# Two-layer AdaLN/MoE block on one core: index loads, ring depth, token layout and the sharing of the head's work

## The reference

```python
x = x + L0_ffn(L0_cond(x, cond))
x = x + L1_ffn(L1_cond(x, cond))

# L0_cond: per sample, a gate picks 2 of 4 experts
gate_in = [mean over all tokens | over head and proprio | over wrist and proprio]
mod = silu(cond) @ time_w + time_b                  # scale, shift
scores = softmax((gate_in @ gate_w + gate_b) * (1 + scale) + shift)
w_be = the two largest scores of the sample, normed to sum 1
for e in range(4):
    y = gelu_tanh(x @ ew1[e] + eb1[e]) @ ew2[e] + eb2[e]     # 128 -> 512 -> 128
    out += w_be[:, e] * mask[e] * y                          # mask: which tokens
out += gelu_tanh(x @ sw1 + sb1) @ sw2 + sb2                  # shared expert

# L0_ffn: all 8 experts, 128 -> 512 -> 128, silu(x @ w_gate) * (x @ w_up) @ w_down,
#         weighted by softmax(router) * softmax(gating / 0.1), normed
# L1_cond: 2 shared experts, 8 routed ones (top 2 of a sigmoid), 128 -> 128 -> 128
# L1_ffn: low rank, gelu(x @ U1 @ V1 + b1) @ U2 @ V2 + b2
```

## Time and profile before

| what | us |
|---|---|
| median of three runs | 980.28 |
| lowest, highest | 978.11, 985.54 |
| the profiled execution, whole | 976.85 |
| its span, first to last instruction | 975.1 |
| PE busy | 906.2 |
| DVE, ACT, POOL busy | 711.7, 564.0, 385.8 |

### The profile page before, as it was taken

The page is one execution under the profiler, slowest core; times in us unless marked ns, Lnnn a source line. Parts: engine busy times, 40 slices in busy tenths (PEclk is TensorE's granted clock), DMA queues, the critical chain, the costliest instruction groups (busy, mean ns, idle before and its releaser), DMA issues.

```text
span 975.1 us, 13047 instructions
## 1 busy us (share of the span) xinstructions
PE 906.2 (93%) x3862; PEld 718.9 (74%) x3862; DVE 711.7 (73%) x1096; ACT 564.0 (58%) x972; POOL 385.8 (40%) x355
## 2 busy tenths in 40 slices
PE   6887777788999999999999999999999999999997
PEld 4665555566788888888888888888888778777884
DVE  6765565564778786866866867768666698898988
ACT  5554444454665554555555555555555658898896
POOL 3602343331134556423523534435222315773551
PEclk8899999996999999999999999999999999999999
DMA  7256676740211131110011011101100019283840
GB/s 272 109 157 184 203 229 203 201 143 1 79 46 76 44 123 54 44 76 11 34 76 44 1 76 43 66 11 44 44 18 26 1 27 174 66 159 57 173 98 33
DMA packets 47671, 85.94 MB, mean 88 GB/s; under 512 B 4208, under 2 KB 26608, under 8 KB 45680
## 3 DMA queue, kind: packets, MB, share of 16 engines
q1 hardware_dynamic: 47600, 85.10, 29.9%
HBM read 68.57 MB, written 6.55 MB: 77 GB/s over the span
## 4 chain that ended last, share of the span: by engine, by line
PE 72%; SPq 8%; DVE 5%; issue 5%; DMA 4%; ACT 4%; POOL 0%; POOLq 0%; DVEq 0%; ACTq 0%
PE ps L772 15%; PE ps L777 15%; PE ps L787 15%; PE ps L817 7%; PE ps L824 7%; PE ps L822 7%; SPq L638 3%; DMA GWU<-expert_weights 3%; SPq L633 2%; PE ps L804 2%; PE ps L802 2%; DVE HL L1304 1%; ACT HH L906 1%; SPq L630 1%; PE ps L698 1%
## 5 line engine op out<-in xcount | busy, mean ns | idle before, releaser
L900 ACT ACTIVATE Sg<-ps 128x512 f32<-128x512 f32 x288 | 172.3, 599 | 250.1 <-PE ps L787 248.8
L1285 DVE TENSOR_TENSOR Hf<-ps,Sg 128x512 f32<-128x512 f32 x288 | 198.0, 688 | 150.6 <-ACT Sg L900 96.6
L1383 POOL TENSOR_TENSOR HL<-Hf,HH 128x512 fp32r<-128x512 f32 x130 | 174.0, 1345 | 165.0 <-ACT HH L906 152.9
L906 ACT ACTIVATE HH<-Hf 128x512 fp32r<-128x512 f32 x346 | 215.9, 624 | 12.8 <-DVE Hf L1285 7.4
L1304 DVE TENSOR_TENSOR HL<-Hf,HH 128x512 fp32r<-128x512 f32 x242 | 217.1, 897 | 4.3 <-ACT HH L906 3.3
L772 PE MATMUL ps<-XHL,WBH 128*128 128x512 f32 x512 | 204.5, 399 | 1.7 <-DVE Hf L1285 1.7
L787 PE MATMUL ps<-XHL,WBH 128*128 128x512 f32 x512 | 202.5, 396 | 0.0
L777 PE MATMUL ps<-XHL,WBL 128*128 128x512 f32 x512 | 202.5, 395 | 0.0
L1402 POOL TENSOR_TENSOR XT<-XT,TMP 128x512 f32<-128x512 f32 x64 | 83.5, 1305 | 255.3 <-DVE TMP L1190 255.3
L1304 DVE TENSOR_TENSOR HL<-ps,HH 128x512 fp32r<-128x512 f32 x120 | 82.6, 691 | 83.5 <-ACT HH L906 80.9
L772 PEld LDWEIGHTS ps<-XHL,WBH 128*128 128x128 f32 x512 | 96.4, 188 | 25.5 <-DVE Hf L1285 3.0
(11 more groups left out here) (242 smaller groups left out, 1383.6 us busy)
## 6 DMA issues: line engine op xcount, KB each, us to landing
CWB<-scratch SPq DMA_DIRECT2D x68, 256.0 KB, 6.8
CWB<-scratch SPq DMA_DIRECT2D x15, 1024.0 KB, 4.6
GX<-XHL SPq DMA_DIRECT2D x76, 128.0 KB, 2.8
GWU<-expert_weights SPq DMA_DIRECT2D x19, 512.0 KB, 3.6
GWD<-expert_weights SPq DMA_DIRECT2D x19, 512.0 KB, 4.9
ST<-in_wb_dram SPq DMA_DIRECT2D x8, 768.0 KB, 6.4
XT<-in_x_dram SPq DMA_DIRECT2D x8, 256.0 KB, 6.2
expert_weights<-GWU SPq DMA_DIRECT2D x4, 512.0 KB, 2.6
```

The costliest lines, as they stand in the source:

```text
L900: e.activation(Sg[:, it.n % NG, :], zb[z % NZ][:, :], ACT.Silu).then_inc(s_act, 1)
L906: e.activation(HH[:, it.n % NH, 0:it.cols], hidden_place(it), ACT.Copy).then_inc(s_hi_act, 1)
L1285: e.tensor_tensor(Hf[:, it.n % NS, :], zb[z % NZ][:, :], Sg[:, it.n % NG, :], ALU.mult).then_inc(s_prod, 1)
L1383: e.tensor_tensor(HL[:, it.n % NH, :], Hf[:, it.n % NS, :], HH[:, it.n % NH, :].bitcast(F32), ALU.subtract).then_inc(s_lo_pool, 1)
```

## The change

- Token parts lie beside each other: `XHL` is [block, part, 512] in place of [part, block, 512], and while it holds x it is used as `XS`, [sample, part, 128], so that both parts of a sample are one run of 1,024 B. `GX` has the same form.
- `GX`, `GWU`, `GWD` become rings of three (`NR`); `GP` is gone: its biases and the mask stand behind the weights in DRAM rows (`wup_d` rows of 1028 numbers, `wdown_d` of 1153), put there by two DRAM-to-DRAM copies in the head.
- `index` is [group, 9]: four samples for the copies, the expert, and four places for the additions. Numbers are loaded four at a time, without a range check, one group ahead; unused places of a group add to spare columns of `AC` (`AC` has 36 samples' width in place of 32), and the waits between POOL's additions are gone.
- The head: Silu is computed with tanh; a small gelu at the very start loads the table of the head; POOL takes ACT's casts of the expert weights; ACT takes the end of A units 0 to 5 from DVE (line 1169 before) and casts the high part of three of four A and G items in place of one of two; the small inputs come in two transfers; the sums over x stand one in each of slots 4 to 9; the other steps of `gates` move to other slots; the loads may begin at slot 19.
- `route_a`: blocks 0 to 3 together at slot t_g + 3 (before: 0, 1 at t_g + 2, 2, 3 at t_g + 3), blocks 4, 5 at t_g + 7 (before t_g + 6).
- `Hf` and `Sg` change places in memory.

The diff, cut to its core:

```diff
-PK = 133
+UROW = 1024 + 4
+DROW = 1024 + 1 + P
+NR = 3
...
-        XHL = sb("XHL", [P, 2, NBLK, BLK], F32R)
-        XH, XL = XHL[:, 0, :, :], XHL[:, 1, :, :]
+        XHL = sb("XHL", [P, NBLK, 2, BLK], F32R)
+        XH, XL = XHL[:, :, 0, :], XHL[:, :, 1, :]
+        XS = XHL[:, :, :, :].rearrange("p b a (s t) -> p (b a s t)", t=P).rearrange("p (s a t) -> p s a t", a=2, t=P)
         sm = sb("sm", [P, SMALL])
...
-        index = sb("index", [P, NPAIR + NGRP], mybir.dt.int32)
+        index = sb("index", [P, NGRP, 9], mybir.dt.int32)
...
-        GX = sb("GX", [P, 2, 2, BLK], F32R, actx)
-        AC = sb("AC", [P, NBLK, BLK], F32, actx)
+        GX = sb("GX", [P, NR, 4, 2, P], F32R, actx)
+        AC = sb("AC", [P, NB + 4, P], F32, actx)
         WAS = sb("WAS", [P, 2, 2, 512], F32R, actx)
-        GWU = sb("GWU", [P, 2, 2, 512], F32R, actx)
-        GWD = sb("GWD", [P, 2, 2, 512], F32R, actx)
-        GP = sb("GP", [P, 3, PK], F32, actx)
+        GWU = sb("GWU", [P, NR, UROW], F32R, actx)
+        GWD = sb("GWD", [P, NR, DROW], F32R, actx)
...
-        route_a = {t_g + 2: (0, 1), t_g + 3: (2, 3), t_g + 6: (4, 5), t_a[6] + 5: (6,), t_a[7] + 3: (7,)}
+        route_a = {t_g + 3: (0, 1, 2, 3), t_g + 7: (4, 5), t_a[6] + 5: (6,), t_a[7] + 3: (7,)}
...
-        first_load = 20
+        first_load = 19
...
-            it.hi_act = it.kind in "BS" or (it.kind in "AGF" and it.k % 2 == 1) or (it.kind == "R" and it.ex % 4 != 3)
+            it.hi_act = it.kind in "BS" or (it.kind in "AG" and it.k % 4 != 0) or (
+                it.kind == "F" and it.k % 2 == 1) or (it.kind == "R" and it.ex % 4 != 3)
...
-        load_x = {pos["G", g - 2, 0, 3].k + 1: g for g in range(2, NGRP)}
-        load_d = {pos["G", g - 2, 0, 3].k + LAG + 1: g for g in range(2, NGRP)}
+        load_x = {pos["G", g - NR, 0, 3].k + 1: g for g in range(NR, NGRP)}
+        load_d = {pos["G", g - NR, 0, 3].k + LAG + 1: g for g in range(NR, NGRP)}
...
-            e.dma_start(sm[:, :], small_d).then_inc(f_sm, 16)
+            e.dma_start(sm[:, 0:SOON], small_d[:, 0:SOON]).then_inc(f_sm, 16)
...
+            e.dma_start(sm[:, SOON:SMALL], small_d[:, SOON:SMALL]).then_inc(f_sm2, 16)
+            e.dma_start(wup_d[:, :, 1024:UROW], pack_d[:, :, 0:4]).then_inc(f_pack, 16)
+            e.dma_start(wdown_d[:, :, 1024:DROW], pack_d[:, :, 4:133]).then_inc(f_pack, 16)
...
-                    w = GWD if h else GWU
+                    d = wdown_d if h else wup_d
+                    w = (GWD if h else GWU)[:, (i - 1) % NR, 0:1024]
                     e.wait_ge(s_wa_lo, 2 * i + h)
-                    e.dma_start(wex_d[i - 1, h], w[:, (i - 1) % 2, :, :].rearrange("p a n -> p (a n)").bitcast(
-                        F32)).then_inc(f_wex[(i - 1) % 2], 16)
+                    e.dma_start(d[i - 1, :, 0:1024], w.bitcast(F32)).then_inc(f_wex[(i - 1) // NR], 16)
                 if k == first_load:
-                    e.wait_ge(s_index, 1)
                     e.wait_ge(s_x_hi, NBLK)
                     e.wait_ge(s_x_lo, NBLK - 1)
-                    e.wait_ge(f_wex[0], 64)
-                    e.wait_ge(f_wex[1], 64)
-                    for g in range(2):
-                        load_tokens(e, g)
-                        load_up(e, g)
-                        load_down(e, g)
+                    e.wait_ge(f_wex[0], 96)
+                    e.wait_ge(f_wex[1], 32)
+                    e.wait_ge(f_pack, 32)
+                    e.wait_ge(s_index, 1)
+                    found = [sources(g) for g in range(NR)]
+                    for g in range(NR):
+                        load_tokens(e, g, found[g])
+                        load_up(e, g, found[g])
+                        load_down(e, g, found[g])
+                    found.append(sources(NR))
                 if k in load_x:
                     g = load_x[k]
-                    e.wait_ge(s_z, pos["G", g - 2, 0, 3].z[0] + 1)
-                    load_tokens(e, g)
-                    load_up(e, g)
+                    e.wait_ge(s_act, pos["G", g - NR, 0, 3].n + 1)
+                    load_tokens(e, g, found[g])
+                    load_up(e, g, found[g])
+                    if g + 1 < NGRP:
+                        found.append(sources(g + 1))
                 if k in load_d:
                     g = load_d[k]
...
+        def indices(engine, g, a, b, most):
+
+            _, v = nc.values_load_multi_w_load_instructions(
+                index[0:1, g, a:b], engines=(engine,), min_val=0, max_val=most,
+                skip_runtime_bounds_check_because="the table counts 32 samples and 4 experts and is clamped")
+            return v
+
+        def sources(g):
+            return indices(mybir.EngineType.SP, g, 0, 4, NB - 1) + indices(mybir.EngineType.SP, g, 4, 5, 3)
+
+        def load_tokens(e, g, v):
             for j in range(4):
-                e.dma_start(GX[:, g % 2, :, j * P:j * P + P].bitcast(F32),
-                            src[:, :, sample_of(e, 4 * g + j), :].rearrange("p a s t -> p a (s t)")).then_inc(
-                                f_gx[g % 2], 16)
-
-        def load_up(e, g):
-            x = expert_of(e, g)
-            e.dma_start(GWU[:, g % 2, :, :].rearrange("p a n -> p (a n)").bitcast(F32),
-                        wex_d[x, 0].rearrange("x p n -> (x p) n")).then_inc(f_gu[g % 2], 16)
-            if g >= 3:
-                e.wait_ge(s_fin, pos["G", g - 3, 0, 3].u + 1)
-            e.dma_start(GP[:, g % 3, :], pack_d[x].rearrange("x p n -> (x p) n")).then_inc(f_gp[g % 3], 16)
-
-        def load_down(e, g):
-            x = expert_of(e, g)
-            e.dma_start(GWD[:, g % 2, :, :].rearrange("p a n -> p (a n)").bitcast(F32),
-                        wex_d[x, 1].rearrange("x p n -> (x p) n")).then_inc(f_gd[g % 2], 16)
+                e.dma_start(GX[:, g % NR, j, :, :].bitcast(F32).rearrange("p a t -> p (a t)"),
+                            XS[:, bass.ds(v[j], 1), :, :].bitcast(F32).rearrange("p s a t -> p (s a t)")).then_inc(
+                                f_gx[g % NR], 16)
+
+        def load_up(e, g, v):
+            e.dma_start(GWU[:, g % NR, :].bitcast(F32),
+                        wup_d[bass.ds(v[4], 1)].rearrange("x p n -> (x p) n")).then_inc(f_gu[g % NR], 16)
+
+        def load_down(e, g, v):
+            e.dma_start(GWD[:, g % NR, :].bitcast(F32),
+                        wdown_d[bass.ds(v[4], 1)].rearrange("x p n -> (x p) n")).then_inc(f_gd[g % NR], 16)
 
         def tensor_program(e):
             e.wait_ge(s_zero, 1)
             for i in range(WARM):
-                mm = e.matmul(ps[NZ - 1][:, :], Hf[:, 0, 0:P], Hf[:, 0, :], start=i == 0, stop=i == WARM - 1)
+                mm = e.matmul(ps[NZ - 1][:, :], AC[:, 4 * FRONT, :], block_sums(FRONT), start=i == 0, stop=i == WARM - 1)
...
+            e.wait_ge(s_zero, 1)
+            e.activation(q1[0:NB, :], AC[0:NB, 4 * FRONT, :], ACT.Gelu_apprx_tanh)
...
-            e.activation(sc[:, :], S("cond"), ACT.Silu).then_inc(s_silu, 1)
+            e.activation(sc[:, :], S("cond"), ACT.Tanh, scale=0.5).then_inc(s_tanh, 1)
-                if k in split_wa:
-                    i, h = split_wa[k]
-                    c = slice(h * 512, h * 512 + 512)
-                    e.wait_ge(f_st[1] if i == 1 else f_wa[i], 16)
-                    if i > 2:
-                        e.wait_ge(f_wex[(i - 1) % 2], 32)
-                    e.activation(expert_weights(i, h)[0], stage_a[i][:, c], ACT.Copy).then_inc(s_wa_hi, 1)
...
+                if LAG <= k < len(items) + LAG and items[k - LAG]:
+                    it = items[k - LAG]
+                    if it.last and it.kind == "A" and it.blk < FRONT:
+                        e.wait_ge(s_down, it.n + 1)
+                        e.activation(block_sums(it.blk), ob[it.u % NO][:, :], ACT.Identity,
+                                     bias=col("sb2")).then_inc(s_fin, 1)
...
-                if k in (2, 4):
+                if 4 <= k <= 9:
+                    h, i = (k - 4) // 3, (k - 4) % 3
                     xv = XT[:, :, :].rearrange("p k n -> p (k n)").rearrange("p (b t) -> p b t", t=P)
-                    for b in range(4 * h, 4 * h + 4):
-                        e.wait_ge(f_x[b], 16)
...
-                    link(e.tensor_scalar(index[0:1, NPAIR:NPAIR + NGRP], q1[0:1, 100:100 + NGRP], 3.0, None, ALU.min))
+                    link(e.tensor_scalar(index[0:1, :, 4], q1[0:1, 100:100 + NGRP], 3.0, None, ALU.min))
+                if k == 18:
+                    table = bj[0:1, 264:264 + NPAIR].rearrange("p (g s) -> p g s", s=4)
                     e.wait_ge(*small.of("table"))
                     after()
-                    e.tensor_copy(index[0:1, 0:NPAIR], bj[0:1, 264:264 + NPAIR]).then_inc(s_index, 1)
-                if k == 18:
+                    link(e.tensor_scalar(index[0:1, :, 0:4], table, float(NB), float(NB - 1), ALU.add, ALU.min))
+                    after()
+
+                    spare = q1[0:1, 0:NPAIR].rearrange("p (g s) -> p g s", s=4)
```

(22 more changed lines are left out.)

198 lines of the change are left out of this document (104 added, 94 removed).

## The result

| what | before, us | after, us |
|---|---|---|
| median (before: 3 runs ahead of the prediction, 4 with the one beside after; after: 4 runs) | 980.28, then 980.23 | 918.63 |
| lowest, highest | 978.11, 985.54 | 916.6, 920.91 |
| the profiled execution, whole | 976.85 | 920.91 |
| its span | 975.1 | 919.0 |

The ratio after / before is 0.9365, interval 0.9321 to 0.9408: faster by 6.35%. The forecast was 918.5.

The account below looks back on a forecast made before the run. SP's own instructions were taken to bound the 19 groups. Gains of 47.3, 6.5 and 6 us (59.8) took the profiled 976.85 to 917.0; about half the median's 3.4 us excess was added for 918.5, range 904 to 934.

Parts of the forecast that it names:

- What bounds the kernel now: In the 19 groups, SP issues without pause, 8.12 us per group; its own instructions are the bound.
- The period: In the groups after the change, PE sets the time per group, 5.55 us.
- SP's 4.4 us: SP's time per group after the change, with two index loads and six issues; bounds 4.1 to 6.1 us.
- SP idle in each group: Expected sign in SP's timeline: SP pauses in every group, waiting for ACT or DVE.
- DMA's 4.9 us: Time to move one group's 1.64 MB after the change, taken between 4.0 and 5.5 us, under PE's 5.55.
- Rival 1: In the groups, copies stay the bound: period about 6.0 to 6.1 us, 9.5 us less gain, 928 us; chance 0.18.
- The main term, 47.3: The 19 groups shrink from 154.8 to 107.5 us, a gain of 47.3 us.
- The head, 6.5: Before the groups, group 0 starts at 53 instead of 59.55 us: gain 6.5, between 0 and 11.
- The single table: In the head, dropping Silu's table switch and the one back starts the first gelu at about 8.1, not 10.7 us.
- The change to the expert stage, 6: Between groups and turn, PE's idle time falls from 4.19 to about 1.4 us; gain 6, or 3 to 9 by clock.
- Rival 3: All goes well: clock holds at the change to the expert stage, group 0 at 51: 912 us; chance 0.15.
- Slower by weight rows off their size: In the groups, weight rows off 4,096 B move at half of 303 GB/s, 9.2 us per group: 988 us; chance 0.03.

Follow-up runs that it names:

- halves apart: After, with high and low token parts in separate halves of XHL and GX again, pieces of 512 B instead of 1,024: 922.14 us, ratio 0.9394.
- first loads in turn: After, with SP reading each of the first three groups' indices just before that group's own copies, not all three ahead: 916.82 us, ratio 0.9328.
- the eight executions of this code: Profiles of after and seven edited kernels with after's exact code behind the groups: rest 753.8 to 757.0 us, stretch 28.4 to 31.4.
- rows on the grid: After, with weight rows padded to pitches of 4,352 and 4,864 B so each starts on a 256 B boundary: 920.63 us, ratio 0.9374.

## Why the prediction was right, and where it was not

- **What bounds the kernel now: right.** SP was the bound of the groups; with a load per transfer put back it is again, at 6.96 us a group without a stop.
- **The period: right.** PE sets it. 5.55 was forecast; 75 / (324 / 24) = 5.56 is measured between 75 and 150 us (one group takes 5.79), and the average of 5.67 from group 0 to 18 holds the 2 us at the start that the prediction had.
- **SP's 4.4 us: mis-sized, 5.02.** The step that failed is "I take 4.4, since a load is one instruction with one round trip": four registers take 0.87 against 0.27 for one. The rule that the prediction took from the Trainium skill, "Runtime: NRT & Kernel Launch", on TENSOR_LOAD, gave 5.0 us, near the 5.02. It speaks of loads from HBM, and these come from the chip's own memory: 0.87 is 0.2 us for each further register, (0.87 - 0.27) / 3, and the median of 0.99 is 0.24, but the 19 loads run from 0.39 to 1.39, so this is no fixed price. And a new token copy costs 0.51 to issue, not 0.35. GWU, with one piece per partition too, takes 0.45 here and 0.35 with a load per transfer, for the same rows; why is open. Under PE's 5.56 both errors cost nothing. "SP idle in each group" did not hold for all: see the groups from 113.43 on.
- **DMA's 4.9 us: a little low, 5.1.** Longer pieces and three groups in flight did raise the rate, as the prediction had it: while busy, the engines move 321 GB/s, 303 before, and 310 with the halves apart. 1.64 MB at 321 take 5.1 us, where 4.9 would need 335. Other transfers of these 75 us (one of 768 KB for the next stage) bring the busy time to 0.95 x 5.56 = 5.3 per group. Rival 1 was not far: about 5% more transfer time and DMA would be the bound.
- **The main term, 47.3: right, 47.2,** and neither half would have brought it: with rings of two 28.6 us are left of it (154.75 - 126.14), with a load per transfer 19.9 (154.75 - 134.89).
- **The head, 6.5: mis-sized, 4.5.** The chains were right: the last link of the index was put at 44.8 and stands at 44.83; POOL's last split was put at 44.4 and ends at 43.05, with the wait for the write-out at 2.79 where 3 was said. What failed is the sum behind it, "44.8 + 2.4 + 2.1 + 0.2 + 3.6 = 53.1": the six loads and the gap before the first copy are 3.4 (48.48 - 45.05; the three of four registers take 0.51, 0.87 and 0.87), the copies with their gaps 2.7, the flight 3.7. Also, what it took as one possible bound, PE's slots at about 50, is at 53, as the kernel with the first loads in turn shows; with it in the way no cheaper index would have brought more than 2 us.
- **The single table: no use here.** The prediction had it start the first gelu at 8.1 and it starts at 7.52; the time was lost again at 18.09.
- **The change to the expert stage, 6: 4.4.** The idle time before the routes was put at 1.4 and is 1.12. The clock, left open, fell: 32 routes take 6.15 where two runs of 16 at full clock take 3.7. That is the case that the prediction priced at 3, and 4.4 came (4 to 7 in the eight executions of this code). Its reason for the fall, "PE now has a gap of 1.4", does not suffice: with the routes one slot later there is no gap and the clock still goes down. The part that needs no clock is right: from the turn on the time is as before, 725.1 us against 724.8.
- **The sum: part luck.** By pieces 3.7 us less was gained than forecast. The median hit (918.63 for 918.5) because I put the median 1.5 above the profiled execution, and it lies 2.3 below: an error of 3.8 against one of 3.7. The range (904 to 934) held both. (Rival 3's 912 is 913.5 by its own terms: 2 us of the head and 3 of the stage change under 918.5.)
- **Slower by weight rows off their size:** nothing of it; GWU lands in 5.4 us, and rows on the grid bring no time.

## What to carry to other kernels

When a queue engine is the bound, write out its group by prices in place (from issue to issue, not the length of one instruction), and then do the same sum for the next two resources: here the change without its ring depth, or without its index loads, would have brought 40 to 60% of what all of it did. At a stage's boundary, place what needs the result of a slow chain a slot later rather than early with a wait: the turn one slot later brought 5 us of the median, about as much as the whole rework of the head. Moving narrow matmuls apart with wide ones between kept the granted clock up in the one kernel that did it without idle time before them; that it saves time by itself is not shown. When an edit of one dictionary moves another task with it, as the softmax moves the turn here, run the second move alone too. An instruction that may wait for a transfer belongs on the engine that nobody waits for at that time.

## What the runs showed of the hardware that was not expected

- An uninterrupted run of 32 matmuls of 16 columns (3.64 us at full clock, PE busy before, in and behind it) was followed by a granted clock of 0.77 over 7 us; the same 32 as two runs of 16 with matmuls of 512 columns between kept 1.00. Each of the two is one profile; the mean granted clock of the whole execution was 0.985 to 0.989 in the four runs of the first and 0.991 to 0.993 in those of the second. Two runs of 16 behind idle time (2.50 us with the routes as before, and 4.19 before the change) had half clock all the same. How long such a run may be was not tried. In eight executions of the same code here the fall came at different times, and the stretch was 28.4 to 31.4 us long.
- A TENSOR_LOAD from the chip's own memory takes 0.27 us for one register on SP. For four it takes 0.39 to 1.39, median 0.99 (19 loads of after); on POOL the load of four has a median of 0.96.
- Copies on chip are issued in 0.51 us for 128 pieces of 1,024 B and 0.62 for 256 of 512 B; 128 rows of 4,112 B take 0.45, and 0.35 in the kernel with a load per transfer.
- DMA at a share of 0.95 over 75 us hardly delayed PE: it was busy 74.95 us of them, though GWU landed in 5.4 us and GWD in 5.9.
- Token copies in pieces of 1,024 B raised what the DMA engines move while busy in this mix from 310 to 321 GB/s (22.53 MB at a share of 0.97, 22.87 at 0.95, over 75 us each); by the same working the other kernels with such pieces lie at 318 to 330.
